# A third complement per head, subtracted by GpSimd, in a 16-head masked attention

## The reference, cut to what matters

```
seq    = (x @ W_seq).reshape(2048, 16, 32)
score1 = einsum('nhd,d->hn', seq, a1)
score2 = einsum('nhd,d->hn', seq, a2)
scores = leaky_relu(score1[:, :, None] + score2[:, None, :], 0.2)
scores = scores + (1.0 - adj)[None] * -65500.0
attn   = softmax(scores, axis=-1)
hidden = einsum('hij,jhd->ihd', attn, seq).reshape(2048, 512)
```

## Time and profile before

| | us |
|---|---|
| median of 3 runs | 2241.11 (2238.02 to 2244.28) |
| the profiled execution, its own time | 2243.45 |
| its span, first to last instruction | 2241.7 |
| attention, from ScalarE's first mask tile to the last L765 | 121.8 to 619 |
| one head in the steady part, L765 of a half 1 to the next one | 29.4 |

### The profile page before, as it was taken

The page is one execution under the profiler, slowest core; times in us unless marked ns, Lnnn a source line. Parts: engine busy times, 40 slices in busy tenths (PEclk is TensorE's granted clock), DMA queues, the critical chain, the costliest instruction groups (busy, mean ns, idle before and its releaser), DMA issues. The chain is left out here.

```text
span 2241.7 us, 38750 instructions
## 1 busy us (share of the span) xinstructions
PE 1948.9 (87%) x15925; PEld 1709.7 (76%) x15925; DVE 1308.1 (58%) x1708; ACT 1084.1 (48%) x1128; POOL 413.3 (18%) x318
## 2 busy tenths in 40 slices
PE   5859999999965359999936879949999999999998
PEld 4859999999953149999925767728888888888886
DVE  7799888888567337777769223443334344343342
ACT  4699888887155225555411023315345344353441
POOL 1022222221020320000055410254101011011011
PEclk9979999999988779999968989979999999999999
DMA  6443233323200457777565431245345253352433
GB/s 245 155 154 105 101 96 105 100 73 26 96 5 1 158 202 249 244 245 251 193 200 177 147 86 38 89 110 159 87 131 141 92 144 90 123 137 95 131 94 118
DMA packets 147573, 290.93 MB, mean 130 GB/s; under 512 B 15819, under 2 KB 52811, under 8 KB 143296
## 3 DMA queue, kind: packets, MB, share of 16 engines
q1 hardware_dynamic: 133184, 256.96, 35.4%
q0 software_dynamic: 14272, 32.28, 5.5%
HBM read 227.18 MB, written 70.71 MB: 133 GB/s over the span
## 5 line engine op out<-in xcount | busy, mean ns | idle before, releaser
L811 PE MATMUL attn_acc<-heads_vals,gat_adj 128*128 128x99 bf16 x2048 | 284.4, 209 | 0.0
L2163 DVE TENSOR_TENSOR moe_w_lo<-moe_raw,moe_w_hi 128x2048 fp32r<-128x2048 f32 x64 | 146.8, 2294 | 233.6 <-ACT moe_w_hi L2120 233.6
L809 PE MATMUL attn_acc<-heads_vals,one_x 128*128 128x99 bf16 (+1 forms) x2048 | 239.9, 230 | 18.3 <-DVE one_x L723 10.9
L809 PE MATMUL attn_acc<-heads_vals,heads_mask 128*128 128x99 bf16 (+1 forms) x2048 | 238.1, 229 | 0.0
L2120 ACT CAST moe_w_hi<-moe_raw 128x2048 fp32r<-128x2048 f32 x64 | 122.2, 1909 | 206.8 <-PE moe_y_ps L2088 192.7
L684 ACT ACTIVATE heads_mask<-gat_s_row,heads_big_s 128x2048 fp8e4<-128x2048 f32 x104 | 197.8, 1989 | 32.3 <-PE attn_acc L811 32.3
L809 PEld LDWEIGHTS attn_acc<-heads_vals,one_x 128*128 128x128 fp8e4 x2048 | 197.5, 98 | 19.6 <-issue 18.2
L811 PE MATMUL attn_acc<-heads_vals,attn_below 128*128 128x99 bf16 x2048 | 203.7, 211 | 2.5 <-issue 2.5
L684 ACT ACTIVATE one_x<-gat_s_row,heads_big_s 128x2048 fp8e4<-128x2048 f32 x101 | 192.1, 1989 | 26.0 <-PE attn_acc L811 26.0
L198 PE MATMUL moe_h_ps<-moe_x_hi,moe_w_hi 128*128 128x512 f32 x512 | 200.0, 391 | 1.6 <-DVE moe_x_lo L2168 1.6
L199 PE MATMUL moe_h_ps<-moe_x_lo,moe_w_hi 128*128 128x512 f32 x512 | 199.7, 390 | 0.0
(11 more groups left out here) (339 smaller groups left out, 4677.9 us busy)
## 6 DMA issues: line engine op xcount, KB each, us to landing
moe_raw<-in_L_ffn_W_dram SPq DMA_DIRECT2D x64, 1024.0 KB, 5.2
moe_wg<-in_L_ffn_w_gate_dram SPq DMA_DIRECT2D x23, 768.0 KB, 6.2
moe_wu<-in_L_ffn_w_up_dram SPq DMA_DIRECT2D x23, 768.0 KB, 7.8
moe_wd<-in_L_ffn_w_down_dram SPq DMA_DIRECT2D x23, 768.0 KB, 9.3
gat_s_row<-s_rows SPq DMA_DIRECT2D x16, 1024.0 KB, 6.3
sym_a<-in_adj_dram SPq DMA_DIRECT2D x32, 512.0 KB, 4.1
one_seq<-sent SPq DMA_DIRECT2D x23, 512.0 KB, 3.6
back<-one_seq SPq DMA_DIRECT2D x46, 256.0 KB, 2.1
```

The costliest lines, as they stand in the source:

```text
L809: mm = pe.matmul(o[:, 0:first], mask[u][:, j, cols], both[:, 0:first], start=(j == 0 and b % 2 == 0), stop=(j == NT - 1), skip_group_check ...
L811: mm = pe.matmul(o[:, 3 * C1:6 * C1], second, both[:, 3 * C1:6 * C1], start=False, stop=(j == NT - 1), skip_group_check=True)
L2163: dve.tensor_tensor(w_lo[n % 2][:], raw[:, n % R], w_hi[n % 2][:], ALU.subtract).then_inc(w_low, 1)
```

## The change

`SPLIT` becomes the quads 1, 2 and 3. The complement of quads 1 and 3 (`OWN`) stays with VectorE's XOR. That of quad 2 is made by GpSimd as a 32-bit subtraction, adjacency minus mask (the mask's bits are a subset of the adjacency's), into buffer 1 of `below`. The three buffers now belong to the three quads, so each complement of head h+1 waits for the use of the same quad's complement of head h. VectorE's two flips move: that of quad 1 comes after both of the second pair of quads, before the combine of half 1; that of quad 3 comes after that combine, at the start of the next head's round. GpSimd makes its complement behind `prepare`, once quad 2 of head h+1 is masked and tile 11 of head h is used up; for head 0 it makes it ahead of the first `prepare` of the loop (the one for head 1).

```
-    SPLIT = (1, 3)
+    SPLIT = (1, 2, 3)
+    OWN = (1, 3)
...
+            def flip(h, u):
+                q = 2
+                pool.tensor_tensor(below[:, 1].rearrange("p t n -> p (t n)").bitcast(I32),
+                                   adj8[:, 4 * q:4 * q + 4, :].rearrange("p t n -> p (t n)").bitcast(I32),
+                                   mask[u][:, 4 * q:4 * q + 4, :].rearrange("p t n -> p (t n)").bitcast(I32),
+                                   ALU.subtract).then_inc(flipped_p, 1)
+
             def head(h, u):
                 pool.wait_ge(half_done, START + 2 * h)
                 pool.sem_inc(passed_p, 1)
                 prepare(ch, seq, ea, eb, vals, h + 1, 1 - u)
                 pool.sem_inc(parts_ready, 1)
-
+                pool.wait_ge(masked, NT + NQ * h + 3)
+                pool.sem_inc(passed_p, 1)
+                pool.wait_ge(mask_used, h * (NT - 1) + 12)
+                pool.sem_inc(passed_p, 1)
+                flip(h + 1, 1 - u)
+
+            pool.wait_ge(masked, NT - NQ)
+            flip(0, 0)
...
-                    if q in SPLIT:
+                    if q in OWN:
                         flip(0, q)
...
                 apply(h, 4 * q, 4)
-                if q in SPLIT:
-                    flip(h, q)
...
             for h in range(H):
+                if h:
+                    flip(h, 3)
                 for half in range(2):
                     if h + 1 < H:
                         masks(h + 1, 2 * half)
                         masks(h + 1, 2 * half + 1)
+                        if half:
+                            flip(h + 1, 1)
                     combine(h, half)
...
-                        if half == 0 and j % 4 == 0 and f is not None:
-                            pe.wait_ge(flipped, f + 1)
+                        if half == 0 and j % 4 == 0 and q in OWN:
+                            pe.wait_ge(flipped, len(OWN) * h + OWN.index(q) + 1)
+                        elif half == 0 and j % 4 == 0 and q in SPLIT:
+                            pe.wait_ge(flipped_p, h + 1)
```

More of the change, by code:

```diff
@@ L638, in attention @@
         stepped, compared, masked, flipped = c.sem("stepped"), c.sem("compared"), c.sem("masked"), c.sem("flipped")
+        flipped_p = c.sem("flipped_pool")
         mask_used, half_done, acc_free = c.sem("mask_used"), c.sem("half_done"), c.sem("acc_free")
```

## The result

The kernel before has a median of 2241.01 us over nine runs (2238.02 to 2248.40), the changed one 2254.58 us over nine runs (2250.78 to 2257.51). The ratio is 1.0057, with a 95% interval of 1.0044 to 1.0071: 13.6 us slower. The profiled execution of the changed kernel took 2250.78 us, with a span of 2249.0 us and a mean granted TensorE clock of 0.943. In its code the subtraction is L696, the comparison L728, the AND L739, VectorE's flip L747, the combine L779, L784 and L785, the matmuls L829 and L831; `prepare` keeps L585 and L590.

A forecast was written before the change was run, and what follows sets the result against it. TensorE bounds the kernel before, VectorE the changed one. Head 0 +4.2, 14 rounds x 1.1 (15.4), last round -1.4 and the end -1.3 make +16.9 us on 2241.1: 2258.0 us, 8 in 10 from 2230 to 2285.

The forecast's parts named there:

- TensorE's part: Quad 2 of each half falls from 4.32 to 3.03 us, making a head 26.8 us in TensorE's own time.
- The subtraction: GpSimd's added complement of quad 2 was taken at 4.4 us, with bounds of 3.8 and 6.75.
- rival 3: GpSimd's integer subtraction goes by a slower path, 6.75 us or beyond: 2275 to 2296 us or more; chance 0.10.
- rival 2: Nothing to measure: the subtraction costs VectorE 3 to 3.6 us, total 2235 to 2247 us; chance 0.14.
- The round: Steady attention head: VectorE's stalls make it 26.1 us plus the subtraction's 4.4, 30.5 instead of 29.4.
- Rival 1: Faster: the subtraction runs while VectorE doesn't need the port, round 26.8 us, total 2205 us; chance 0.22.
- Head 0: First head: prepare moves to the last four ANDs and a comparison waits for the subtraction; flip ends at 158.0, 4.2 us later.
- The end: Last round ends with TensorE's 28.0 us, 1.4 less; the split quad and half behind it take 16.4 for 17.7, 1.3 less.
- The sum: Whole kernel: 4.2 + 14 rounds x 1.1 (15.4) - 1.4 - 1.3 = +16.9 us.
- TensorE's clock: Lower clock after TensorE's gaps in each round: costed at nothing as flip waits cover it; without cover 14 us.
- partial form: Faster case where only VectorE's reduction covers 1.8 us of the subtraction: round 28.7 us, total 2233 us.

The follow-up runs named there:

- skip: Changed kernel with GpSimd subtracting for head 0 only, heads 1 to 15 reusing that complement: 2208.00 us against 2241.65 for the kernel before, ratio 0.9842.
- unsplit_b: Changed kernel with quad 2 left unsplit on TensorE, which still waits for GpSimd's unread complement: 2256.19 us against 2241.36 for the kernel before.
- memset: Changed kernel with GpSimd's subtraction replaced by a memset of the same 8192 bytes, same waits: 2205.09 us against 2241.65 for the kernel before.
- half: Changed kernel with GpSimd's subtraction cut to 1024 words in heads 1 to 15: 2225.14 us against 2241.65 for the kernel before, ratio 0.9927.
- moved: Kernel before with only VectorE's two flips in the changed order, nothing added to GpSimd: 2242.04 us against 2243.36, ratio 0.9997.
- dve3_two: Changed kernel with VectorE making all three complements and, in heads 1 to 15, tile 11 on ScalarE: 2228.66 us against 2243.36 for the kernel before.

## Why the prediction was right, and where it wasn't

It forecast 2258.0 us, 16.9 more than before; it is 2254.58, 13.6 more, for the reason given. By the interval of the ratio the difference is 9.9 to 15.9 us, so 16.9 is a little too much. Step by step:

**TensorE's part.** A round of 26.8 in TensorE's own time was forecast; `skip` has 26.75. It is the one part that shows nothing in the changed kernel, as `unsplit_b` tells.

**The subtraction.** Taken at 4.4 us, from a GpSimd product that had begun inside a VectorE instruction. From the end of the AND it takes 4.41 above; the shortest of its 16 rows is 4.53. The lower bound, 3.8 from L590, was too low, and the upper, 6.75, was L334's waiting counted as work. The Trainium skill's 4497 ns for an f32 add of the same size (GPSIMD Engine Reference, 3.1) agrees with the 4.53. The integers take no slower path, so rival 3 falls; rival 2 would have needed a cost of 3 to 3.6 us.

**The round.** The prediction counted from the end of an AND at 15.4; here that is 417.12.

| after that AND, us | forecast | in the trace |
|---|---|---|
| the subtraction ends | 4.3 | 4.41 |
| flip of quad 1 ends | 6.5 | 6.56 |
| L585 both done | 8.6 | 8.59 |
| the combine's subtraction ends | 11.1 | 11.03 |
| flip of quad 3 ends | 15.1 | 15.03 |
| the round | 30.5 | 30.44 |
| TensorE's two waits | 1.1 and 2.5 | 1.1 and 2.3 |

The rule from which all these follow (two-operand instructions on the two engines exclude each other and take turns) was read from the earlier trace rows; `memset` adds that a GpSimd instruction which only writes is no part of it. On VectorE's side the rule is too narrow. The comparison L728 has one tensor operand and waits as well: two of them take 6.73 us for 2.48 beside the subtraction of head 0, and one takes 2.97 for 1.28 beside an L590 that ran from 248.23 to 252.01 (both rows below). The prediction let the last comparison of head 0 wait, without a row for it, and was right. The reduction stays the one that is seen to run unharmed.

**Rival 1** said that the sign turns where the subtraction costs VectorE under 3.3 us. `half`, with 2.17, came out faster by 0.73%, and its round of 28.25 lies where 26.1 + 2.17 puts it.

**Head 0.** VectorE's timeline of it, to set against the earlier trace rows:

```profile
128.72 2.48 DVE L739 TENSOR_TENSOR one_x<-one_x,gat_adj 128x512 int32<-128x512 int32 x4
...
141.85 6.73 DVE L728 TENSOR_SCALAR one_x<-gat_s_row,heads_ns 128x2048 fp8e4<-128x2048 f32 x2
148.50 7.82 DVE L739 TENSOR_TENSOR one_x<-one_x,gat_adj 128x512 int32<-128x512 int32 x4
156.36 2.29 DVE L747 TENSOR_TENSOR attn_below<-gat_adj,one_x 128x2048 int32<-128x2048 int32 x1
```

The first four ANDs fell from 7.82 to 2.48 us, the last four rose from 2.50 to 7.82, the comparisons before them wait for the subtraction (6.73 for 2.48), and the flip ends at 158.65. The forecast was 158.0; the stage's first comparison starts 0.6 us later in this execution, so the step is right to 0.05.

**The end.** The last round was forecast at 28.0 us, set by TensorE, with a split quad and a half (16.4) behind it. The last two reductions:

```profile
615.64 1.81 DVE L779 TENSOR_REDUCE attn_sums<-attn_acc 128x528 f32<-128x1584 f32 x1 [6.60 <-PE attn_acc L831]
...
629.01 1.81 DVE L779 TENSOR_REDUCE attn_sums<-attn_acc 128x528 f32<-128x1584 f32 x1 [10.63 <-PE attn_acc L831]
```

Both wait for TensorE. 629.01 - 16.4 = 612.6, and the flip of quad 3 before that round ended at 584.05 (579.98 + 4.07 in the timeline): 28.5 us. That this is near 28.0 is luck. The forecast was TensorE's own time and a wait of 1.1 us for the flip of quad 1. In the trace that flip ended at 601.68, before TensorE began that head at 602.08, and TensorE did not wait for it. What it lost instead stands at the start of the round, in its first split quad and the first matmul behind it:

```profile
584.20 0.20 PE L829 MATMUL attn_acc<-heads_vals,one_x 128*128 128x99 bf16 x1 [2.08 <-DVE attn_below L747]
...
588.70 0.25 PE L829 MATMUL attn_acc<-heads_vals,one_x 128*128 128x198 bf16 x1
```

4.50 us for a quad that takes 3.03, 1.5 lost, at a granted clock of 0.67 from 584 to 587 us and 0.76 in the next 3 us.

**The sum** is the step that is off. In the two profiled executions the attention's last reduction moves from 617.22 to 629.01, by 11.8, not 16.9. From the flip of head 0 to that reduction the prediction's rounds give 14 x 30.5 + 28.0 + 16.4 = 471.4 after the change; the trace has 629.01 - 158.65 = 470.4. For the kernel before they give 15 x 29.4 + 17.7 = 458.7; its trace has 617.22 - 153.8 = 463.4, 4.7 more. Thus 16.9 + 0.6 (later start) - 1.0 - 4.7 = 11.8. The term that was mis-sized is the old kernel's: the one gap with its stretch at a granted clock of 0.56 was seen and left out of the old rounds, so each of them was taken as steady. VectorE's timeline before has that round, 33.59 us, 4.2 more than 29.4:

```profile
524.80 1.81 DVE L765 TENSOR_REDUCE attn_sums<-attn_acc 128x528 f32<-128x1584 f32 x1 [2.49 <-PE attn_acc L811]
...
558.39 1.81 DVE L765 TENSOR_REDUCE attn_sums<-attn_acc 128x528 f32<-128x1584 f32 x1 [2.53 <-PE attn_acc L811]
```

It is no accident of one execution: `moved`, whose rounds TensorE sets too, has a gap of 2.76 us and a round of 33.86 in the same head. The changed kernel has gaps of 0.97 and 2.13 us there, at 549.59 and 555.49, and its rounds don't show them, because VectorE sets them: the two rounds around the gaps take 60.6 us together, twice 30.3. What TensorE waited for in these gaps the profile doesn't show (it lists them as issue). The rest of the pair, 7.3 us between the two profiled executions instead of 11.8, lies behind the attention: 1624.5 us before, 1620.0 after, which no step of the change touches; over the twelve traces this part varies from 1620.0 to 1626.1.

**TensorE's clock** was costed at nothing. In the mean that held: the fourteen rounds of the trace from 158.65 to 584.05 (end of a flip of quad 3 to the next) are 30.39 us each. Where no wait covers it, as in the last round, a stretch at the lower clock costs 1.5 us, more than the 0.95 that was read from a window of 3 us. And the rounds are not alike. Three times a short and a long one stand beside each other, 26.7 and 33.9. Before the first of them TensorE had waited 2.1 us for a flip, and the granted clock fell, as the second window shows. The first window is of the round ahead of it, where the clock fell as well:

```profile
189.00:192.00 3.00, 2.76 (x34) 2.79 (x35) 3.00 (x3) 1.64 (x1) 0.00 (x0) 0.51 0.02 5
...
219.00:222.00 3.00, 2.34 (x30) 2.37 (x31) 3.00 (x3) 0.73 (x1) 0.00 (x0) 0.63 0.02 5
```

0.63 is a mixture of the two levels, 1.2 and 2.4 GHz; 0.51 is all but the lower one. After the like gap of the round shown first the clock stayed at 1.00, and the subtraction began 13.85 us into the round, inside an AND. After a fall of the clock TensorE is later with tile 11, and the subtraction begins 15.1 to 15.35 us into the round, close to the 15.34 at which VectorE's flip begins. In the three such rounds where it was 0.09 us or more ahead of the flip (the one from 189.09 is one of them) it went first, and the round took 30.4. In the four where the two began within 0.02 us of each other, the flip went first; three of these are the short ones, the fourth is the last round. The first of the four, in GpSimd's and VectorE's timelines:

```profile
234.87 6.70 POOL L696 TENSOR_TENSOR attn_below<-gat_adj,heads_mask 128x2048 int32<-128x2048 int32 x1 [17.50 <-PE attn_acc L831]
```

```profile
234.86 2.29 DVE L747 TENSOR_TENSOR attn_below<-gat_adj,heads_mask 128x2048 int32<-128x2048 int32 x1
237.74 1.81 DVE L779 TENSOR_REDUCE attn_sums<-attn_acc 128x528 f32<-128x1584 f32 x1 [0.60 <-PE attn_acc L831]
239.59 2.27 DVE L784 TENSOR_TENSOR attn_num<-attn_sums,heads_g 128x264 f32<-128x264 f32 x1
...
246.15 4.04 DVE L739 TENSOR_TENSOR one_x<-one_x,gat_adj 128x2048 int32<-128x2048 int32 x1
250.11 2.97 DVE L728 TENSOR_SCALAR one_x<-gat_s_row,heads_ns 128x2048 fp8e4<-128x2048 f32 x1
...
262.82 6.52 DVE L739 TENSOR_TENSOR one_x<-one_x,gat_adj 128x2048 int32<-128x2048 int32 x1
```

The flip took 2.29 us and the subtraction ran beside a wait, the reduction and the combine's multiplication, which took 2.27 us for 0.43: that is rival 1 for one round, in its partial form. Then `prepare` came late and fell on the next round's AND (4.04) and comparison (2.97), and the subtraction after it on an AND (6.52). 26.7 + 33.96 = 60.7, twice 30.3. The stalls move, their total stays. So a fall of the clock alone doesn't make a short round; it brings the two starts together, and a few hundredths of a us decide the order. This is read from seven rounds of one trace and was not tested.

**Not seen** in the prediction: the loop through the combine and the flip behind it. It did no harm in the changed kernel, where VectorE's stall is longer, but it would have made a cure by a lighter VectorE alone fail, as `dve3_two` did.

## What to carry to other kernels

Before a two-operand elementwise step is handed to GpSimd because GpSimd is idle, price what it takes from VectorE: here 4.35 us of stall for a step that VectorE does itself in 2.3. When one engine's busy share reads 99%, compare its instructions with their durations alone, since waits for the other engine are listed as work. And when taking work off the full engine moves nothing, look for a loop through two engines, and move the instruction that one of them waits for ahead of the one that waits itself.

## What the runs showed of the hardware that was not expected

- A GpSimd memset of 4096 two-byte elements per partition, 3.51 us, costs a two-operand VectorE instruction beside it nothing (2.28 us), where a subtraction of the same bytes costs it 4.35.
- VectorE's comparison, which has one tensor operand, is held up by GpSimd's two-operand instructions too: 2.97 us for 1.28 beside an L590. The reduction is not.
- The exclusion can change phase. Where the subtraction and VectorE's flip began within 0.02 us of each other, which they did only in rounds that start at a lower granted clock, the flip went first, and three times a round of 26.7 us was followed by one of 33.9.
